# Two gated cross-attention blocks: query, head, attended and output products in groups of two steps on TensorE

## The reference, cut to what matters

```python
qn = layernorm(x, ln_q_g, ln_q_b)
q = qn @ Wq * scale                      # 256 -> 1024 = 16 heads x 64
k, v = split(media @ Wkv)                # 128 -> 2 x 1024
sim = einsum('bhid,bhjd->bhij', q, k)    # masked by media_mask
out = einsum('bhij,bhjd->bhid', softmax(sim), v)
x = x + tanh(attn_gate) * (out @ Wo)     # 1024 -> 256
h = layernorm(x, ln_ff_g, ln_ff_b)
x = x + tanh(ff_gate) * (gelu(h @ W1) @ W2)
```

## Time and profile before

| | us |
|---|---|
| median of the runs shown | 1474.73 |
| the profiled execution, its own time | 1476.38 |
| its span in the trace | 1474.6 |
| TensorE (PE) busy | 1403.8 (95%) |
| VectorE busy | 906.7 (61%) |
| ScalarE busy | 581.3 (39%) |
| GpSimd busy | 553.7 (38%) |

### The profile page before, as it was taken

One profiled execution on the slowest core, in us unless ns is written; L12 is line 12 of the kernel. 1 busy time (PEld: TensorE's weight loads), 2 busy tenths in 40 slices (PEclk: granted clock), 3 DMA queues, 4 the chain that ended last, 5 costly groups with the idle time before them and its releaser, 6 DMA issues.

```text
span 1474.6 us, 20618 instructions
## 1 busy us (share of the span) xinstructions
PE 1403.8 (95%) x7850; PEld 740.6 (50%) x7851; DVE 906.7 (61%) x1429; ACT 581.3 (39%) x880; POOL 553.7 (38%) x385
## 2 busy tenths in 40 slices
PE   6979899999999989998998999999999999999998
PEld 3446555555555544444654455555344355555344
DVE  6896766666667616421226788887433778888540
ACT  1264366666666652001442344444122434444121
POOL 2630388888888891000001144452000144453000
PEclk9999999999999999999999999999999999999999
DMA  7000623232323204004842011110042001110000
GB/s 274 0 2 20 165 70 90 67 92 71 88 66 92 52 13 191 0 0 174 335 124 71 0 39 39 40 39 1 0 122 70 1 27 39 39 39 13 1 0 25
DMA packets 45019, 95.62 MB, mean 65 GB/s; under 512 B 6860, under 2 KB 28892, under 8 KB 44908
## 3 DMA queue, kind: packets, MB, share of 16 engines
q1 hardware_dynamic: 44912, 94.21, 21.0%
HBM read 72.04 MB, written 0.97 MB: 50 GB/s over the span
## 4 chain that ended last, share of the span: by engine, by line
PE 84%; DVE 8%; POOL 3%; issue 2%; ACT 2%; DMA 0%; SPq 0%; DVEq 0%; ACTq 0%; POOLq 0%
PE psum L1658 23%; PE psum L2175 10%; PE psum L1899 5%; PE psum L1875 5%; PE psum L1849 4%; PE psum L2107 4%; PE psum L1832 3%; PE psum L2138 3%; PE psum L1818 3%; POOL XN L708 3%; PE psum L2165 2%; PE psum L2170 2%; DVE WA L1341 2%; PE psum L2167 2%; PE psum L2166 2%
## 5 line engine op out<-in xcount | busy, mean ns | idle before, releaser
L1341 DVE TENSOR_REDUCE WA<-psum 112x2 f32<-112x1000 f32 x192 | 229.8, 1200 | 89.9 <-PE psum L1849 89.9
L708 POOL TENSOR_TENSOR XN<-XN,WBZ 125x896 f32<-125x896 f32 x128 | 266.5, 2082 | 16.8 <-POOL XN L708 0.9
L1052 ACT ACTIVATE WA<-psum,y_bias 125x448 f32<-125x448 f32 x192 | 118.6, 633 | 208.9 <-PE psum L2170 190.4
L933 ACT ACTIVATE WBZ<-psum 125x896 f32<-125x896 f32 x192 | 175.5, 915 | 43.9 <-PE psum L1875 33.3
L2175 PE MATMUL psum<-WA,ctxN 125*128 125x448 f32 x384 | 180.9, 554 | 0.8 <-ACT WA L1052 0.7
L740 POOL TENSOR_TENSOR XN<-const,y_max 112x896 bf16<-112x896 f32 x32 | 75.2, 2350 | 246.2 <-DVE y_max L1557 189.2
L731 POOL TENSOR_SCALAR ctxT<-ctxT 128x375 f32<-128x375 f32 x32 | 56.2, 1756 | 250.9 <-ACT std L806 248.4
L1557 DVE CUSTOM_DVE_ANT_0 XA<-psum,WA 112x375 bf16<-112x375 f32 x240 | 125.3, 541 | 37.6 <-PE psum L2138 36.6
L1875 PE MATMUL psum<-R 100*125 100x224 f16 x768 | 110.7, 266 | 0.0
L1570 DVE RECIPROCAL WBZ<-WBZ 128x224 f32<-128x224 f32 x68 | 105.1, 1546 | 0.1
L1875 PEld LDWEIGHTS psum<-R 100*125 100x125 f16 x768 | 78.9, 136 | 28.3 <-issue 25.0
(11 more groups left out here) (255 smaller groups left out, 2337.9 us busy)
## 6 DMA issues: line engine op xcount, KB each, us to landing
R<-WA SPq DMA_DIRECT2D x192, 93.8 KB, 2.2
WA<-in_ctxT SPq DMA_DIRECT2D x14, 750.0 KB, 4.3
ctxT<-in_ctxT SPq DMA_DIRECT2D x11, 750.0 KB, 4.2
ctxN<-in_ctx SPq DMA_DIRECT2D x32, 192.0 KB, 2.5
ctxT<-in_ctxT SPq DMA_DIRECT2D x32, 187.5 KB, 2.4
R<-in_ctx SPq DMA_DIRECT2D x7, 768.0 KB, 7.3
R<-in_ctxT SPq DMA_DIRECT2D x7, 750.0 KB, 7.2
WA<-in_ctx SPq DMA_DIRECT2D x6, 768.0 KB, 6.4
```

What stands on the lines that cost most here:

```text
L708: nc.gpsimd.tensor_tensor(z_sum[b % 2][0:TK, :], first[0:TK, :], z_p[t % 4][0:TK, :], ALU.add)\
L933: nc.scalar.activation(z_p[t % 4][0:TK, :].rearrange("p (k n) -> p k n", k=2), psum[0:TK, s:s + 2, 0:2 * GC], ACT.Exp, scale=float(CHD0) * ...
L1052: nc.scalar.activation(y_pT[t][0:TK, g * HALF:(g + 1) * HALF], bank[2 + u % 3][0:TK, 0:HALF], ACT.Exp, bias=y_bias[0:TK, bass.ds(b * NT + ...
L1341: V.tensor_reduce(z_mx[0:PR, r:r + 3:2, c], psum[0:PR, lo:lo + 2, 0:PC], AX_X, ALU.max)\
```

## The change

In both loops of PE, and in the DVE and schedule loops that mirror them, the steps are taken two at a time: two query products (or two steps of attended products), then the head products (or output products) of the two steps before. Four places of `XA` are used in place of two (`attended_at`: steps with m % 4 of 2 or 3 use the other half's columns), since two steps' results now stand while the next two are written. What is put between moves with it: on PE it comes right after its query or attended product, on DVE in `queries` after the head parts of its group. The norm of the second half is put later: PE's variance from step 2 to 4, ACT's square ahead of all heads and its root from after head 5 to after head 3, DVE's inverse roots from steps 3 and 4 to 4 and 5, its scale from 5 to 6.

```diff
@@ schedule()
-            for m in range(XT + 1):
-                if m < XT:
+            for g in range(XT // 2 + 1):
+                for m in range(2 * g, min(2 * g + 2, XT)):
                     ev.add(("q", l, h, m), "dve")
-                if m >= 1:
-                    for j in range(2):
-                        ev.add(("qk", l, h, 2 * (m - 1) + j), "dve")
+                for head in range(max(4 * g - 4, 0), 4 * g):
+                    ev.add(("qk", l, h, head), "dve")
...
+        def attended_at(m, h):
+            return XA[:, m % 2, half(h if m % 4 < 2 else 1 - h)]
@@ ACT
-                    queries(l, 0, {0: lambda: square("nq", l, 1), 2: lambda: root("nq", l, 1)})
+                    square("nq", l, 1)
+                    queries(l, 0, {1: lambda: root("nq", l, 1)})
@@ DVE queries
-                for m in range(XT + 1):
-                    if m < XT:
+                for g in range(XT // 2 + 1):
+                    for m in range(2 * g, min(2 * g + 2, XT)):
                         src = take(dve, ("q", l, h, m))
...
-                    if m >= 1:
+                    for k in range(max(2 * g - 2, 0), 2 * g):
                         for j in range(2):
-                            head = 2 * (m - 1) + j
+                            head = 2 * k + j
...
-                    if m in between:
-                        between[m]()
+                    for m in range(2 * g, min(2 * g + 2, XT)):
+                        if m in between:
+                            between[m]()
@@ DVE gated
-                    queries(l, 0, {0: lambda: centre("nq", l, 1), 3: lambda: inverse_root("nq", l, 1, 0),
-                                   4: lambda: inverse_root("nq", l, 1, 1), 5: lambda: scale("nq", l, 1, 0, 1)})
+                    queries(l, 0, {0: lambda: centre("nq", l, 1), 4: lambda: inverse_root("nq", l, 1, 0),
+                                   5: lambda: inverse_root("nq", l, 1, 1), 6: lambda: scale("nq", l, 1, 0, 1)})
@@ PE queries
+                for g in range(XT // 2 + 1):
+                    for m in range(2 * g, min(2 * g + 2, XT)):
                         product(("q", l, h, m), [(features(x_wq[:, k], m), XN[:, k, half(h)]) for k in range(KD)])
-                    if m >= 1:
-                        emptied(pe, ("q", l, h, m - 1))
+                        if m in between:
+                            between[m]()
+                    for k in range(max(2 * g - 2, 0), 2 * g):
+                        emptied(pe, ("q", l, h, k))
                         for j in range(2):
                             rows_j = slice(HDX * j, HDX * (j + 1))
-                            product(("qk", l, h, 2 * (m - 1) + j),
-                                    [(x_wkT[rows_j, m - 1, :], XA[rows_j, (m - 1) % 2, half(h)])])
-                    if m in between:
-                        between[m]()
+                            product(("qk", l, h, 2 * k + j), [(x_wkT[rows_j, k, :], attended_at(k, h)[rows_j])])
@@ PE projected
+                for g in range(XT // 2 + 1):
+                    for m in range(2 * g, min(2 * g + 2, XT)):
                         n, bk, engine, count, old = ev.at[("av", l, h, m)]
...
-                    if m in between:
-                        between[m]()
-                    if m >= 1:
-                        k = m - 1
+                        if m in between:
+                            between[m]()
+                    for k in range(max(2 * g - 2, 0), 2 * g):
                         emptied(pe, ("av", l, h, k))
@@ PE gated
-                    queries(l, 0, {0: lambda: query_mean(l, 1), 2: lambda: half_variance("nq", l, 1)})
+                    queries(l, 0, {0: lambda: query_mean(l, 1), 4: lambda: half_variance("nq", l, 1)})
```

More of the change, by code:

```diff
@@ L1478, in queries @@
             def queries(l, h, between):
-                for m in range(XT + 1):
-                    if m < XT:
+                for g in range(XT // 2 + 1):
+                    for m in range(2 * g, min(2 * g + 2, XT)):
                         src = take(dve, ("q", l, h, m))
                         some = (anys[:, HB * h:HB * (h + 1)].rearrange("p (b o) -> p b o", o=1).to_broadcast([P, HB, S]))
-                        inc_empty(V.tensor_tensor(by_seq(XA[:, m % 2, half(h)]), by_seq(src[:, 0:HT]), some, ALU.mult))
-                    if m >= 1:
+                        inc_empty(V.tensor_tensor(by_seq(attended_at(m, h)), by_seq(src[:, 0:HT]), some, ALU.mult))
+                    for k in range(max(2 * g - 2, 0), 2 * g):
                         for j in range(2):
-                            head = 2 * (m - 1) + j
+                            head = 2 * k + j
                             dve.wait_ge(sem("q_high"), 2 * HEADS * l + HEADS * h + head + 1)
@@ L1498, in projected @@
                     inverse = y_den[:, 1 + HB * h:1 + HB * (h + 1), m * S:(m + 1) * S]
-                    inc_empty(V.tensor_tensor(by_seq(XA[:, m % 2, half(h)]), by_seq(src[:, 0:HT]), inverse, ALU.mult))
+                    inc_empty(V.tensor_tensor(by_seq(attended_at(m, h)), by_seq(src[:, 0:HT]), inverse, ALU.mult))
                     if m in between:
@@ L2107, in projected @@
                             mm = pe.matmul(bank[4 + 2 * h + mo][:, 0:HT], features(x_wo[:, k], mo),
-                                           XA[:, k % 2, half(h)], start=(k == 0), stop=(k == XT - 1))
+                                           attended_at(k, h), start=(k == 0), stop=(k == XT - 1))
                             if k == XT - 1:
```

## The result

The kernel after takes 1480.90 us (median of 7 runs, 1479.95 to 1481.92), the one before 1474.73 (7 runs, 1470.37 to 1476.30): a ratio of 1.0044, with a 95% interval of 1.0031 to 1.0058. It is slower by 6.2 us. The profiled execution took 1481.09 us with a span of 1479.3.

The account below looks back on a forecast made before the run. TensorE (PE), 84% of the chain that ended last, was taken to bound the kernel. Projections -3.5, queries +8.4 and clock +1.6 made +6.5 us on a median of 1474.7: 1481.2 us, range 1476 to 1486.5.

Parts of the forecast that it names:

- Projections: Both halves of both blocks' projections: fewer alternations at 0.34 us each, two blocks gain 3.5 us.
- The wait ahead of the variance: Projections, half 1: PE reaches the variance before the square is done and waits 0.7 us.
- Queries, second half: Second half of each block's queries, product 0 to walk: 28.1 us against 25.2, a loss of 2.9 us per block.
- the rotation of four banks: Queries: four heads fill banks 0 to 3, so PE idles 0.7 us before query product 4.
- the score's wait: Queries, second half: the early score behind product 4 waits 0.44 us for maximum 2, taken after four low parts.
- Queries, first half: First half of the queries: a smaller loss, 1.9 us in block 0 and 0.7 us in block 1.
- Its layout of the order of before: Step-by-step timing of the ungrouped queries' first half: 26.7 us in block 0, against 28.6 after the change.
- Clock: Long PE idles ahead of second halves and walks: one more clock fall than now, 1.6 us lost.
- The norm's 'two steps later': Queries, first half: the second half's norm placed later gains nothing, since nobody waits for the variance.
- POOL's step: Ahead of the walk: POOL's 1.68 us step after the last maximum stays hidden, with 0.6 us left.
- A: Rival: only alternations count; queries gain 6.4 us and projections 4.9, giving 1463.4 us; chance 0.08.
- C: Rival: clock falls at all four idles in the blocks, +9.7 us, giving 1484.4 us or more; chance 0.15.

Follow-up runs that it names:

- a1: The kernel before with only the projections grouped in pairs of steps, queries unchanged: 1469.21 us, ratio 0.9962 to before.
- b2: The kernel after with query and head products rotating over six banks in place of four: 1478.77 us, ratio 1.0032 to before.
- b1: The kernel after with DVE's two early maxima of a group ahead of its four low parts in the second half: 1477.74 us, ratio 1.0025 to before.
- b4: b1 with ACT's table load after head 7 in place of head 11: 1474.06 us, a single execution.
- f1: c2 with unread TensorE products filling idles ahead of second halves, walks and the blocks' start: 1466.08 us, ratio 0.9943 to before.
- f2: The kernel before with grouped projections, their variance after step 5, and unread products ahead of walks and the blocks' start: 1467.99 us, ratio 0.9958 to before.
- d1: The kernel after with the second half's norm sooner: variance, inverse roots and scale at their former steps, root after head 1: 1481.31 us, ratio 1.0049 to before.
- a2: The kernel after with the projections of before, so only the queries grouped, with the later norm: 1484.74 us, ratio 1.0071 to before.
- c2: The kernel after with six banks, early maxima first, table load after head 7 and the projections' variance after step 5: 1471.69 us, ratio 0.9981 to before.
- e1: The kernel after with unread TensorE products filling PE's idles ahead of the second half and the walk: 1477.63 us, ratio 1.0027 to before.

## Why the prediction was right, and where it was not

The forecast of 1481.2 us came within 0.3 us. Its direction and its two large terms came for its reasons; that it came so close is partly luck, as the interval of the measurement alone is 4 us wide and two of the steps below were off. Step by step:

- **Projections, -3.5 forecast, -3.6 measured** (2 x 1.8, and the same in a1). One alternation at 0.34 us from the earlier trace rows carried over: half 0 of block 0 takes 19.84 us in place of 21.23, 1.4 less as laid out. The wait ahead of the variance was 0.57 us in place of 0.7.
- **Queries, second half, +2.9 per block forecast, +2.81 measured** (28.03). Two steps came to 6.64 us against 6.6. Single waits were each a little shorter than laid out: 0.53 in place of 0.7 ahead of product 4, 0.28 in place of 0.44 ahead of the score.
- **What was wrong in that step** is which of the waits counts. The prediction put the loss to the rotation of four banks first and treated the score's wait as a rest. Six banks (b2) leave the half at 28.06; the maxima in front (b1) give 1.12 back, the table load (b4) 0.88. The rotation matters only once the others are gone: 26.03 in b4 goes to 24.60 with six banks (f1), another 1.43.
- **Queries, first half, +1.9 and +0.7 forecast.** The traces have +0.39 and +0.76, but in block 0 before the change the clock had fallen. With the same queries and no fall (f2) that half takes 25.80, so the change costs 2.08 there. In sum the queries lose 2.08 + 0.76 + 5.62 = 8.5 us at an equal clock, against 8.4. Here two errors cancelled. The prediction took 0.6 us for the low clock at the start of block 0, the row of product 0 alone, where it cost 1.7 (27.49 against 25.80). Its layout of the order of before, 26.7 for that half, was therefore 0.9 too long and seemed to fit; that of after, 28.6, was 0.7 too long (27.88).
- **Clock, +1.6 forecast.** The walk of block 0 did fall, +1.60. In this pair of traces the fall at block 0's start went away at the same time (-1.7), which is why the spans differ by 4.7 and not 6.4. So this term did not come in the pair of traces: each has two falls. It was a count over three idles, and with 22 falls behind 43 unfilled idles the odds were about even. What the medians leave for it, 6.2 less 8.5 plus 3.6, is 1.3 us, and no run attributes it. The medians differ by 6.2, with an interval of 4.6 to 8.6 us; single executions of before lie 5.9 us apart, those of after 2.0, so one pair of traces can't settle it.
- **"The norm's 'two steps later' gains nothing: nobody waits for the variance" was wrong.** It was read from the trace of before, where heads stand ahead of the variance. Grouped, they don't: with the early place PE waits 1.25 us for the square (d1). The first half takes 29.32 in place of 27.80 in block 1 and, the low clock taken off, 28.1 in place of 27.88 in block 0. Most of the 1.5 us in block 1 goes with the table load, which the later root lets ACT take in an idle; that gain the prediction did have, in its +0.7 for block 1. The times of d1 and after don't differ.
- **POOL's step was hidden with 0.6 us left**, forecast and measured (0.57).

Of the rivals, A (only the alternations count) fell for this kernel: a2 is 10 us slower than before. It has a true core, seen in f1: with these waits away the grouped second half takes 24.60 us against 25.22. That is 0.6 us, where A counted on 1.6, and in block 0 the first half takes it back. The Trainium skill, "TensorEngine Tiling", Key Properties, has the rule that changing the tiling mode drains the engine. The traces agree that a change costs, with 0.34 us for one alternation (there and back) in the projections; whether a drain is the reason, no run here shows. What fewer changes give is had only where the results find their reader in time. C (the clock falls at every idle) did not come in after itself: of its four idles of 1.65 and 2.24 us, the two ahead of the walks were followed by a fall and the two ahead of the second halves were not. In c2 three of those four places had one. The Trainium skill, "TensorE: Matmul & The Clock Gate", "A second HAM failure mode: psum-queue depth-cycling", puts such swings down to short idles between groups that cycle through banks. In the blocks no run here shows a fall behind the waits between the groups, which are of 0.3 to 1.2 us (up to 1.61 in d1), only behind the idles of 1.65 us and more ahead of a stage.

## What to carry to other kernels

Grouping products of one form pays by the alternations that go, and it asks the reader for the results in bursts. So before grouping, lay out the reader's way from the first result of a burst to the first free bank, with all that stands on that engine between, and move its side work (here the maxima, a table load) to where it waits anyway. A group that changes what stands ahead of an instruction also changes who waits for it: the place of everything put between has to be read anew, as the variance shows in the projections (0.57 us of waiting) and in d1 (1.25 us). Where PE had to idle for some 2 us ahead of a stretch that it bounds, no fall came behind products that nobody reads, and a fall costs 1.6 us or more. It came behind about half of the idles: the filling gained about 3 us in e1 and 5 to 6 in f1, and nothing that the times show in f2.

## What was not expected of the hardware

- **The same idle is followed by a fall of the clock in one trace and not in another.** Second half of block 1 after 1.65 us of idle: first product 1.74 us in after and 3.31 in a2. Walk of block 1 after 1.83 us: granted clock 0.60 before, no fall in a1. Walks after 2.24 us: a fall at both in after, at none in d1. Most falls cost 1.6 to 1.7 us; that at the first walk of b1 cost 2.9 (190.69 against 187.77, granted clock 0.52 and 0.62 in the two stretches behind its start) and that of b2, after 3.30 us of idle, 2.4. What decides is open: no run varied the length of one idle alone.
- **Four head products in a row take 1.70 us** from the first to the next query product (823.89 to 825.59 in f1), where one pair between query products takes 0.95 (824.11 to 825.06 in the earlier trace rows). The second pair, which brings no change of form, adds 0.75.
- **The table load itself can be had for nothing**: between the high parts of heads 11 and 12 it cost 0.88 us of its 1.28, and in a gap of ACT (b4) nothing that the trace shows.
